# ScalarE's copies and signs and TensorE's scores in another order, two buffers for the similarities, and P copied along tokens

## The reference, cut to what matters

```python
xn = (x - mu) * rsqrt(var + BN_EPS) * gamma + beta            # batch norm
q = (xn @ w_q.T).reshape(b, n, 2, h, kd).transpose(2, 0, 1, 3, 4)
sim = einsum('pbnhd,hkpd->pbnhk', q, keys)                    # 2 x 8 heads x 32 keys
s, i = top_k(sim, 8)                                          # in both halves
all_scores = (sx[..., :, None] + sy[..., None, :]).reshape(b, n, h, 64)
scores, pk = top_k(all_scores, 8)
idx = take_along_axis(all_idx, pk)                            # 8 of 1024 experts a head
o = einsum('bnd,bnhkd->bnhk', inputs, key_in[idx])
o = gelu(o) * softmax(scores)
y = einsum('bnhk,bnhkd->bnd', o, key_out[idx])
out = layernorm(x + y)
```

## Time and profile before

| | |
|---|---|
| median of three executions | 571.52 us |
| the profiled execution, its own time | 576.09 us |
| its span, first to last instruction | 574.3 us |
| mean granted TensorE clock | 0.715 of full speed |
| busy: PE, DVE, ACT, POOL | 371.0, 454.2, 268.1, 239.8 us |
| loop of the second part | from about 95 us to the end |

### The profile page before, as it was taken

The page is one execution under the profiler, slowest core; times in us unless marked ns, Lnnn a source line. Parts: engine busy times, 40 slices in busy tenths (PEclk is TensorE's granted clock), DMA queues, the critical chain, the costliest instruction groups (busy, mean ns, idle before and its releaser), DMA issues.

```text
span 574.3 us, 24195 instructions
## 1 busy us (share of the span) xinstructions
PE 371.0 (65%) x10097; PEld 285.5 (50%) x10097; DVE 454.2 (79%) x2767; ACT 268.1 (47%) x377; POOL 239.8 (42%) x311
## 2 busy tenths in 40 slices
PE   5687685284568648772968395839673866585655
PEld 3233572044365637462747373737463645564544
DVE  2557796999997799889978995899699969994432
ACT  4877523354245535554454345444653545362231
POOL 1043400442851456544755461446354746280300
PEclk9898865675659565965686669666975787586658
DMA  8600000000000000000000000000000000000000
GB/s 232 138 0 2 0 1 1 1 2 3 3 5 2 4 3 22 2 5 21 4 2 3 22 3 3 3 21 5 3 4 22 3 3 2 23 2 5 2 22 19
DMA packets 7644, 8.94 MB, mean 16 GB/s; under 512 B 880, under 2 KB 6896, under 8 KB 7408
## 3 DMA queue, kind: packets, MB, share of 16 engines
q1 hardware_dynamic: 6960, 7.34, 4.8%
q10 hardware_dynamic: 576, 0.07, 0.1%
HBM read 5.31 MB, written 2.10 MB: 13 GB/s over the span
## 4 chain that ended last, share of the span: by engine, by line
PE 47%; DVE 25%; ACT 13%; issue 13%; DMA 1%; SPq 0%; ACTq 0%; POOL 0%; DVEq 0%
PE psum L826 15%; PE psum L803 14%; PE psum L813 9%; ACT arena L411 5%; DVE arena L642 4%; PE psum L722 3%; PE psum L783 3%; DVE idx L587 3%; DVE arena L639 2%; DVE arena L499 2%; DVE arena L646 2%; ACT nat L431 2%; DVE arena L645 2%; DVE x L549 1%; DVE picked L611 1%
## 5 line engine op out<-in xcount | busy, mean ns | idle before, releaser
L803 PE MATMUL psum<-arena 64*64 64x16 f16 x8192 | 114.4, 193 | 135.8 <-issue 55.2
L803 PEld LDWEIGHTS psum<-arena 64*64 64x64 f16 x8192 | 108.4, 142 | 149.7 <-issue 99.9
L411 ACT ACTIVATE arena<-psum 128x1024 f32<-128x1024 f32 x32 | 61.0, 1905 | 121.0 <-PE psum L803 121.0
L826 PE MATMUL psum<-ko,arena 64*128 64x128 f32 x1024 | 93.6, 360 | 3.7 <-issue 3.7
L826 PEld LDWEIGHTS psum<-ko,arena 64*128 64x128 f32 x1024 | 89.9, 271 | 5.0 <-issue 4.6
L587 DVE FIND_INDEX8 idx<-vals,sims 128x8 uint32<-128x32 f32 x512 | 82.7, 205 | 0.0
L282 POOL TENSOR_TENSOR arena<-arena 128x512 f32<-128x512 f32 x60 | 74.4, 1270 | 15.4 <-ACT arena L411 15.4
L642 DVE TENSOR_TENSOR arena<-iota,listsT 128x4096 f16<-128x4096 f16 x32 | 77.0, 2405 | 0.0
L235 POOL TENSOR_TENSOR cand<-vals 128x128 f32<-128x128 f32 x16 | 7.3, 458 | 138.3 <-DVE vals L579 138.3
L813 PE MATMUL psum<-x1T,trn 128*64 128x256 f32 x512 | 59.3, 385 | 7.0 <-ACT arena L417 7.0
L579 DVE MAX8 vals<-sims 128x8 f32<-128x32 f32 x512 | 49.3, 193 | 12.5 <-ACT sims L377 12.3
(11 more groups left out here) (106 smaller groups left out, 581.8 us busy)
## 6 DMA issues: line engine op xcount, KB each, us to landing
x<-in_L_attn_x_dram SPq DMA_DIRECT2D x8, 256.0 KB, 4.8
out_dram<-nat SPq DMA_DIRECT2D x8, 256.0 KB, 2.1
ko<-in_L_ffn_key_out_dram SPq DMA_DIRECT2D x2, 512.0 KB, 10.0
nat<-in_L_ffn_key_in_dram SPq DMA_DIRECT2D x2, 256.0 KB, 8.5
nat<-in_L_ffn_keys_dram SPq DMA_DIRECT2D x2, 128.0 KB, 5.6
nat<-in_L_attn_W_delta_dram SPq DMA_DIRECT2D x1, 64.0 KB, 2.8
nat<-in_L_attn_W_in_dram SPq DMA_DIRECT2D x1, 64.0 KB, 2.7
nat<-in_L_attn_W_select_dram SPq DMA_DIRECT2D x1, 64.0 KB, 2.8
```

The source lines that it names most:

```text
L411: act.activation(dst, src, ACT.Copy, scale=1.0 / W_SCALE).then_inc(s["p_evac"], 1)
L803: end = pe.matmul(psum[64 * e:64 * e + 64, at:at + NJ], hotx[rows, g, :, e], hotw[rows, part, g, :, e], start=(part == 0), stop=(part == 1))
L826: end = pe.matmul(y2[:, e, m % 2], gl[rows, m % 4, j, :], ko[rows, j, :], start=(j == 0), stop=(j == NJ - 1))
```

## The change

Five edits:

- TensorE: `scores(m+1)` moves from behind `lists_turned(m-1)` to the head of iteration m, ahead of `experts_out(m-3)`. At the end of the loop `experts_out(NS-2)` moves ahead of the last two `scatter`s.
- `sims` gets two buffers, so `sims_out(m)` waits for the indices of step m-2 rather than m-1; DVE's `greatest` gets a wait for its own earlier instructions.
- ScalarE: `sims_out(m+1)` moves ahead of the Gelus; `signs(m)` moves from the head of iteration m+1 to iteration m, ahead of `p_out(m-1, 0)`.
- ScalarE: `norm_out` of a quarter moves from the even iteration, ahead of `p_out(m-1, 0)`, to the head of the next odd one.
- `p_out` reads and writes in another order: the innermost index was the expert j (16 next to each other in PSUM, 128 words apart in `pn`), and is now the token g (16 words apart in PSUM, next to each other in `pn`).

```diff
-        sims = sb("sims", [P, 2, ROWS, NK])
+        sims = sb("sims", [P, 2, 2, ROWS, NK])
...
             def sims_out(m):
                 for t in range(2):
                     wait(act, "sim_mm", m * 2 + (t + 1))
-                    wait(act, "idx_done", m * 2 - 1 + t)
-                    act.activation(sims[:, t].rearrange("p r k -> p (r k)"), b_sim[t], ACT.Copy).then_inc(
+                    wait(act, "idx_done", m * 2 - 3 + t)
+                    act.activation(sims[:, m % 2, t].rearrange("p r k -> p (r k)"), b_sim[t], ACT.Copy).then_inc(
...
             def p_out(m, hf):
...
-                src = psum[:, b_p * 512:(b_p + 2) * 512].rearrange("p (t g j) -> p t g j", t=2, j=NJ)
-                dst = pn[:, m % 2].rearrange("p j (t g) -> p t g j", t=2)[:, :, 32 * hf:32 * hf + 32]
+                src = psum[:, b_p * 512:(b_p + 2) * 512].rearrange("p (t g j) -> p j t g", t=2, j=NJ)
+                dst = pn[:, m % 2].rearrange("p j (t g) -> p j t g", t=2)[:, :, :, 32 * hf:32 * hf + 32]
...
             for m in range(NS + 1):
-                if m >= 1:
-                    signs(m - 1)
+                if m >= 5 and m % 2:
+                    norm_out(m // 2 - 2)
                 if m >= 2:
                     p_out(m - 2, 1)
...
                 if m >= 1:
                     lists_out(m - 1)
+                if m + 1 < NS:
+                    sims_out(m + 1)
                 if m % 2 and m < NS:
                     gelus(m // 2)
-                if m + 1 < NS:
-                    sims_out(m + 1)
                 if m >= 4 and m % 2 == 0:
                     spread2(m // 2 - 2)
-                    norm_out(m // 2 - 2)
+                if m < NS:
+                    signs(m)
                 if m >= 1:
                     p_out(m - 1, 0)
+            norm_out(NCH - 2)
             p_out(NS - 1, 1)
...
             def greatest(m):
                 for t in range(2):
                     wait(dve, "sims_ready", m * 2 + (t + 1))
+                    wait(dve, "idx_done", m * 2 - 1 + t)
...
             scores(0)
-            scores(1)
             for m in range(NS + 1):
+                if m + 1 < NS:
+                    scores(m + 1)
                 if m >= 3:
                     wait(pe, "lists_evac", m - 1)
                     experts_out(m - 3)
                 if m >= 1:
                     lists_turned(m - 1)
-                if 2 <= m + 1 < NS:
-                    scores(m + 1)
                 if m % 2 and m < NS:
                     experts_in(m // 2)
+                if m == NS:
+                    wait(pe, "lists_evac", NS)
+                    experts_out(NS - 2)
                 if m >= 1:
                     scatter(m - 1, 0)
                     scatter(m - 1, 1)
-            wait(pe, "lists_evac", NS)
-            experts_out(NS - 2)
             experts_out(NS - 1)
```

More of the change, by code:

```diff
@@ L576, in greatest @@
                     wait(dve, "sims_ready", m * 2 + (t + 1))
+                    wait(dve, "idx_done", m * 2 - 1 + t)
                     for r in range(ROWS):
                         p, h = r // H, r % H
-                        end = dve.max(vals[:, p, t * H + h, :], sims[:, t, r, :])
+                        end = dve.max(vals[:, p, t * H + h, :], sims[:, m % 2, t, r, :])
                     end.then_inc(s["vals_done"], 1)
@@ L586, in indices @@
                         p, h = r // H, r % H
-                        end = dve.max_index(idx[:, p, t * H + h, :], vals[:, p, t * H + h, :], sims[:, t, r, :])
+                        end = dve.max_index(idx[:, p, t * H + h, :], vals[:, p, t * H + h, :], sims[:, m % 2, t, r, :])
                     end.then_inc(s["idx_done"], 1)
```

## The result

The changed kernel takes 601.36 us (median of four, 597.53 to 603.61), the kernel before beside it 572.3. The ratio is 1.049, with a 95% interval of 1.042 to 1.056: slower, by 29 us. The profiled execution took 603.61 against 576.09 before, its span is 601.8 against 574.3. Of these 27.5 us 2.6 lie ahead of the loop, which the change does not touch (PE's first scores begin at 98.66, before at 96.03), so the loop has to account for 24.9. The forecast was 582.

What follows compares the result with a forecast made beforehand. PE's in-order queue was taken as the bound. Terms -1.2 + 12.6 + 1 - 1.2 - 1.6 - 3.1 + 4 = +10.5 took the profiled 576.09 to 586.6, the median to 582 us; 8-in-10 range 562 to 602.

Steps and rivals of the forecast that it cites:

- An even iteration: PE, iterations 4 to 14: 25.98 us becomes 25.8, second scatter kept at 4.84; -0.2 each, six give -1.2.
- iteration 16: Middle wait loses 3.0 us, experts_out(14) with 5.1 fills DVE's wait of 4.91: +0.3; together -2.7.
- the six odd ones: PE, iterations 3 to 13: new wait +2.0, copy between scatters -0.6, later Gelu load +0.7; +2.1 each, +12.6.
- The new wait ahead of the scores: PE after the second scatter, iterations 2 to 14: waits for copy and `xn`, 2.0 us, 13 times.
- The copy: ScalarE's copy of P: 1.3 us, between full rate (990 ns) and the old 1905 ns.
- The first rival: ScalarE's copy of P gets no cheaper, 1.9 us; 29 exposed copies lose 0.6 each, +17.5; 599.5 us; chance 0.25.
- +5 at the edge of the range: PE's scatters, eight odd iterations: instruction supply may turn a scatter beginning 0.6 sooner into longer stops, up to +5 us.
- The clock: PE: scores slower at low clock, `experts_out` about 1.0 less; +0.3 us a time, 13 times +4.
- The late Gelus: Odd iterations: `sims_out` puts 1.1 us of copies ahead of ScalarE's Gelu table load; PE waits, +0.7 us each.
- Nothing for the sign and the buffers: DVE's 33.9 us idle ahead of `pack` goes but it waits elsewhere; sign ahead and second `sims` buffer count 0.
- iterations 1 and 2: Iteration 1: cheaper copy, scores fit into the lists wait but Gelu load late, -1.6 us; iteration 2: +1.
- behind it: End of the loop: 8.91 us for two `experts_out` become 1.4 copy, 1.3 DVE multiply, 5.8 for one: -0.4.

## Why the prediction was wrong, point by point

The direction was forecast, the size was not: +10.5 us against +29. The measured 601.36 lies just inside the stated range, at its upper edge. In the loop +10.5 were forecast and 24.9 measured. Of the 14.4 missed, the six even iterations make +15.3, iteration 16 makes +6.1, and the six odd ones -5.9, so errors of both signs partly cancel. The 2.6 us ahead of the loop are no effect of the change: in the fourteen profiled executions the first scores begin anywhere from 94.8 to 98.7.

*The new wait ahead of the scores* was right: 2.0 forecast, 1.67 measured, 13 times, with ScalarE's `xn` at its end.

*The copy* was forecast at 1.3 us and came to 1.02. The Trainium skill ("SBUF — State Buffer", section "Door 1: The DMA port swizzle") gives PSUM lines of 8 bytes and says of matmuls that they slow down when they do not access it contiguously. The prediction read this as a rule for every access, by which the copy would have stayed at 1.9. For ScalarE reading 16 words apart that did not hold, at 1.02. The first rival named the right time, 599.5, and the wrong reason.

*An even iteration* is the step that failed, in the term for the second scatter. I wrote that "the wait of 4.36 falls to the copy alone, 1.4", which it did (1.13), and kept the second scatter at 4.84. It took 6.92 in the mean. Scatter, wait and scatter were 14.2 together and became 13.4; I had booked 3.0 less and 0.8 came. Six times 2.2 is 13 us. What the runs showed in its place is that the second scatter stops for its instructions when it starts sooner: with the two edits that shorten the wait and nothing else it took 7.02. I had seen the limit ("a new run of 128 products began ... 3.8 to 4.0 apart") and charged it to the odd iterations alone, as +5 at the edge of the range, though an even iteration has the same four blocks.

*The clock*: +4 charged, nothing measured over scores and `experts_out` of two iterations together (16.1 against 16.4). Odd iterations gave +1.4 instead of +2.4, as `experts_out` gained more (6.82 to 4.05) than the scores lost (1.73). The late Gelus were right: +0.7 forecast, 8.41 to 9.15 measured.

*Iteration 16*: -2.7 forecast, +3.4 measured (the end of one scatter to the next: 26.1 before, 29.5 changed). "`experts_out(14)` with 5.1 fills DVE's wait of 4.91" overlooked what `experts_out(14)` itself waits for (5.46), and that this wait and its own 6.6 us then stand ahead of the last two scatters.

*Nothing for the sign and the buffers* agrees with the runs: DVE's idle time moved, and the kernel that keeps both has the ratio of the one without them. No run took either alone.

| part of the loop | forecast | measured |
|---|---|---|
| iterations 1 and 2 | -0.9 | -1.9 |
| iterations 3 to 14 | +15.0 | +24.4 |
| iteration 15 | -0.6 | -1.1 |
| iteration 16 | -2.7 | +3.4 |
| behind it | -0.4 | +0.1 |

## What to carry to other kernels

When a stage issues many tiny instructions, look at the distance between the stops in its timeline and count instructions, not only products: where the stream of instructions is the limit, a wait inside that stage is partly or wholly covered by the time that the stream needs to catch up, and removing it gives only the rest (0.8 of 3.1 us in an even iteration here, 0.1 of 0.9 in an odd one). Before an instruction is moved to the head of an in-order queue, follow its input back to the work just ahead of it; here that chain ran through the engine's own last product. And of what is moved into a gap, read every wait, those on buffers to be overwritten too.

## What the runs showed of the hardware

A ScalarE copy of 1024 elements that read PSUM in steps of 64 bytes and wrote SBUF contiguously took 1024 ns. The copy that read contiguously and wrote single words to SBUF 512 bytes apart took 1905 ns, so here the stepped write is what costs. PE's instructions came in packets of 16 KiB, 256 instructions each. Where stops followed each other closely, they ended never less than 3.3 and mostly 3.5 to 4.1 us apart, while 128 products with their weight loads, which are one such block, ran in 1.9. Four wide products right behind a scatter took 3.4 to 3.8 us with or without a pause in between (granted clock 0.50 to 0.56 there, that is mostly 1.2 GHz), and 1.94 behind `experts_out` (1.00, 2.4 GHz).
